# Local attention: maxima subtracted as the bias of eight exponentials per tile instead of by two products on TensorE

## The chip, the core and the metric

The kernel runs on one core of a Trainium2 chip. The metric is the device time of one execution in microseconds (us); the time before is the median of three executions, 1153.07 us (1151.7 to 1158.17). Engines are named as in the profile: PE is TensorE's matmul, PEld its weight load, DVE is VectorE, ACT is ScalarE, POOL is GpSimd, SP is SyncE. L1261 is line 1261 of the kernel before.

## The reference, cut to what matters

A first attention block (16 heads, full softmax over 1024 positions) is followed by two layers that each hold a local attention and a gated MLP. The change lies in the local attention, which is run once in each of the two layers:

```python
def local_attention(q, k, v):          # 8 heads of 64, window 64, sequence 1024, batch 2
    ...
    sim = jnp.einsum('bhwid,bhwjd->bhwij', bq, bk)
    i = bt[:, :, None]
    j = btk[:, None, :]
    mask = (i < j) | (i > j + WINDOW) | (j == -1)
    sim = jnp.where(mask, -jnp.finfo(sim.dtype).max, sim)
    attn = jax.nn.softmax(sim, axis=-1)
    out = jnp.einsum('bhwij,bhwjd->bhwid', attn, bv)
    return out.reshape(b, h, n, d)
```

Each query sees the 128 keys of its own window and the one before it. The softmax of a row needs the row's maximum, the exponentials of the differences and their sum.

## The kernel before

The 2 x 1024 rows are cut into 16 tiles of 128 rows (T = 16). Everything after the first attention block is a software pipeline. `over_tiles` walks through steps; in each step every engine runs its list of stages in the order in which the list is written, and a stage with lag g works on tile (step - g). Nothing else orders the work: an engine is in order, and each stage begins with waits on semaphores that count what other engines have finished.

The local attention of a layer has these lags: `turn_x` 0, `project_qk` and `products` 1, `square` and norms 2, `turn_qk` 3, everything about scores 4, `multiply_v` and `turn_o` 5, `project_out` 6. In one step the engines run, in this order:

- PE: `multiply_qk` (two products of the mask with an identity, L1380, and 32 small score products, L1385), `multiply_v` of the tile before (32 products, L1398), `project_v` (L1411), `shift_scores` (L1418), `project_qk` (L1435), `turn_e` (eight transposes of the exponentials, L1444), `turn_o` (four, L1450), `turn_qk` (eight, L1465), `project_out` (L1474), `turn_x` (L1427).
- ACT: `square` (L1248), `take_v` (L1255), `exponentials` (L1261), `take_eT` (two copies, L1280), `take_oT` (L1296), `take_qkT` (L1286, L1290), `take_hT` (L1271 to L1274).
- DVE: `maxima` (L1317), `normalise`, `weighted`, `square_sums`, `products` (four, L1349), `denominators` (L1354, L1357), `residual` (L1362).

The scores of a tile fill banks 5 and 6 of PSUM: 128 query rows by 8 heads by 128 keys. `maxima` writes the negated maximum of each row and head into `nmax` (128 x 8). `shift_scores` waits for it and adds it to the scores where they lie, by two products that accumulate into the two banks. `exponentials` then waits for `shifted` and turns all 1024 columns in one instruction. `turn_e` waits for `exp_done`, transposes heads 0 to 3 into bank 3 and heads 4 to 7 into bank 4, and `take_eT` copies each bank away once its four transposes are done.

Of the 16 steps of a layer in which scores are computed, the first 13 also have a `project_qk` between `project_v` and `turn_e` (tiles 0 to 12 of the scores); in the last three no projection is left to do. The MLP of a layer starts 17 steps after its attention and overlaps its last steps. Its `gelu` (L1573) has three instructions per tile, each over 128 columns of a PSUM bank, with a bias from an SBUF column and a semaphore of its own.

Of the kernel before, what the change touches and what calls it, by code (L numbers as in the profile page):

```python
# [8 lines left out]
F32R = mybir.dt.float32r  # L9
BF16 = mybir.dt.bfloat16  # L10
ALU = mybir.AluOpType
ACT = mybir.ActivationFunctionType
AX_X = mybir.AxisListType.X

P = 128
B, N, D = 2, 1024, 128
TB = N // P
T = B * TB
# [59 lines left out]
def need(eng, sem, count):  # L78

    if count > 0:  # L80
        eng.wait_ge(sem, count)
# [11 lines left out]
def adaln_block(nc, x, wq, wk, wv, wo, f_wqkv, f_qs, f_ks, f_wo, f_lg, f_lb, f_w1, f_b1, f_w2, f_b2,  # L93
# [7 lines left out]
    with ExitStack() as whole:  # L101
# [919 lines left out]
        mask_b = fsb("mask_b", [P, 2, 2 * WIN], BF16)  # L1021
        ident_b = fsb("ident_b", [P, P], BF16)
        ident_w = fsb("ident_w", [P, 2, WIN], BF16)
        ident_r = fsb("ident_r", [P, P], F32R)
        XS = fsb("XS", [P, T, D // 2])
        buffers = {}

# [43 lines left out]
        with nc.Block() as block:  # L1071
            @block.vector
            def _(dve):
                dve.wait_ge(ld_mask, 16)
                dve.tensor_copy(mask_b[:, :, :], mask[:, :, :])
                dve.tensor_copy(ident_b[:, :], ident[:, :])
                dve.tensor_copy(ident_r[:, :], ident[:, :])
                for w in range(2):
                    half = slice(WIN * w, WIN * w + WIN)
                    dve.tensor_copy(ident_w[half, :, :], ident[half, half][:, None, :].to_broadcast([WIN, 2, WIN]))  # L1080
# [2 lines left out]
        before = {"xf_done": xf_done, "tab_done": tab_done, "res_step": res_step}  # L1083
        for l in range(DEPTH):
            att_sems, attention = local_attention(l, psum, sb, new_sem, dict(before), XF, XA, XS, ident, minus_half,
                                                  fw_qkv, fw_o, xpos[:, l], mask, mask_b, ident_b, ident_w, ident_r)
            before.update(att_sems)
            mlp_sems, mlp = gated_mlp(l, psum, sb, new_sem, dict(before), X, XF, XA, XS, ident, minus_half, fw_1,
                                      fw_2, fb_1, f_ln, rows, out, scale_tables)
            before = {**att_sems, **{name: mlp_sems[name] for name in ("gelu_done", "u_done", "xf_done")}}  # L1090
            parts += [(attention, LAYER_STEPS * l + AHEAD), (mlp, LAYER_STEPS * l + MLP_STEP + AHEAD)]
# [28 lines left out]


def local_attention(l, psum, sb, new_sem, before, XF, XA, XS, ident, minus_half, fw_qkv, fw_o, xpos, mask, mask_b,
                    ident_b, ident_w, ident_r):


    def banks(a, n=1):
        return psum[:, a:a + n, :].rearrange("p b c -> p (b c)")
# [3 lines left out]
    def sem(name):  # L1131
        sems[name] = new_sem(f"{name}_a{l}")
        return sems[name]
# [12 lines left out]
    vp = sb("vp_att", [P, 2, INNER])  # L1146
    qT = sb("qT_att", [P, 2, FH // 2, P])
    kT = sb("kT_att", [P, FH // 2, WIN + N])
    nmax = sb("nmax_att", [P, 2, FH], F32R)
    E = sb("E_att", [P, 2, FH, 2 * WIN])  # L1150
    den = sb("den_att", [P, 2, FH])
    den_inv = sb("den_inv_att", [P, 2, FH])
# [17 lines left out]
    qkT_done = sem("qkT_done")  # L1170
    scores_done = sem("scores_done")
    max_done = sem("max_done")
    shifted = sem("shifted")
    exp_done = sem("exp_done")
    den_done = sem("den_done")
    inv_done = sem("inv_done")
# [63 lines left out]
    def scalar(act):  # L1240
        if l == 0:
            act.wait_ge(cleared, 1)

        def square(t, s):
            need(act, cos_done, 2 * (t + 1))
            need(act, sin_done, 2 * (t + 1))
            need(act, ss_done, t)
            act.activation(sq[:, :, :].rearrange("p h d -> p (h d)"), banks(0, 2), ACT.Square).then_inc(sq_done, 1)  # L1248

        def take_v(t, s):  # L1250
            need(act, v_proj, t + 1)
            need(act, pv_done, t - 1)
            if t > 0:
                act.wait_ge(vp_in[1 - s], 32 * ((t - 1) // 2 + 1))
            act.activation(v[:, s, :], banks(2), ACT.Copy).then_inc(v_done, 1)  # L1255

        def exponentials(t, s):
            need(act, shifted, t + 1)
            need(act, e_turned, 2 * (t - 1))
            need(act, den_done, t - 1)  # L1260
            act.activation(E[:, s].rearrange("p h c -> p (h c)"), banks(5, 2), ACT.Exp).then_inc(exp_done, 1)  # L1261

        def take_hT(t, s):


            need(act, v_proj, t - HR + 1)
            need(act, x_turned, t + 1)
            need(act, hT_done, 3 * t)
            if l > 0 and t == 0:
                act.wait_ge(before["hT_done"], 3 * T)  # L1270
            act.activation(hT[HD:P, t % HR, 0:1], hT[HD:P, (t - 1) % HR, P:P + 1], ACT.Copy,  # L1271
                           scale=0.0 if t % TB == 0 else 1.0).then_inc(hT_done, 1)
            act.activation(hT[0:HD, t % HR, 0:P], ps_x[0:HD, :], ACT.Copy).then_inc(hT_done, 1)
            act.activation(hT[HD:P, t % HR, 1:P + 1], ps_x[HD:P, :], ACT.Copy).then_inc(hT_done, 1)  # L1274

        def take_eT(t, s):
            need(act, pv_done, t - 1)
            for n in range(2):
                need(act, e_turned, 2 * t + n + 1)
                act.activation(ET[:, s, 4 * n:4 * n + 4, :], banks(3 + n).rearrange("p (h c) -> p h c", c=P),  # L1280
                               ACT.Copy).then_inc(eT_done, 1)

        def take_qkT(t, s):
            need(act, qk_turned, 2 * t + 1)
            need(act, scores_done, t - 1)
            act.activation(qT[:, s, :, :], banks(3).rearrange("p (j c) -> p j c", c=P), ACT.Copy)\  # L1286
                .then_inc(qkT_done, 1)
            need(act, qk_turned, 2 * t + 2)
            c0 = WIN + t % TB * P
            act.activation(kT[:, :, c0:c0 + P], banks(4).rearrange("p (j c) -> p j c", c=P), ACT.Copy)\  # L1290
                .then_inc(qkT_done, 1)

        def take_oT(t, s):
            need(act, o_turned, t + 1)
            need(act, out_proj, t - 1)
            act.activation(oT[:, s], banks(7).rearrange("p (j c) -> p j c", c=P), ACT.Copy)\  # L1296
                .then_inc(oT_done, 1)

        return [(square, NORMS), (take_v, SCORES), (exponentials, SCORES), (take_eT, SCORES), (take_oT, PV),
                (take_qkT, TURN_QK), (take_hT, TURN_X)]  # L1300

    def vector(dve):
# [10 lines left out]
        def maxima(t, s):  # L1313

            need(dve, scores_done, t + 1)
            need(dve, shifted, t - 1)
            dve.tensor_reduce(nmax[:, s, :], banks(5, 2).rearrange("p (h c) -> p h c", c=P), AX_X, ALU.max,  # L1317
                              negate=True).then_inc(max_done, 1)

# [29 lines left out]
                    dve.tensor_tensor(dst[:, s, n * FH:(n + 1) * FH, :], ps_qk[n], table, ALU.mult).then_inc(done, 1)  # L1349

        def denominators(t, s):
            need(dve, exp_done, t + 1)
            need(dve, inv_done, t - 1)
            dve.tensor_reduce(den[:, s, :], E[:, s, :, :], AX_X, ALU.add).then_inc(den_done, 1)  # L1354
            need(dve, den_done, t + 1)
            need(dve, o_done, t - 1)
            dve.reciprocal(den_inv[:, s, :], den[:, s, :]).then_inc(inv_done, 1)  # L1357
# [9 lines left out]
    def tensor(pe):  # L1367
        def multiply_qk(t, s):
            need(pe, qkT_done, 2 * (t + 1))
            need(pe, exp_done, t)  # L1370
            if l == 0 and t == 0:
                pe.wait_ge(before["res_step"], 4 * T)
            c0 = t % TB * P
# [37 lines left out]
            pe.matmul(banks(2), hT[:, t % HR, 0:P], fw_qkv[:, l, 2 * INNER:3 * INNER], start=True, stop=True)\  # L1411
                .then_inc(v_proj, 1)

        def shift_scores(t, s):

            need(pe, max_done, t + 1)
            for n in range(2):
                last = pe.matmul(banks(5 + n).rearrange("p (h c) -> p h c", c=P), ident_r[:, :],  # L1418
                                 nmax[:, s, 4 * n:4 * n + 4][:, :, None].to_broadcast([P, FH // 2, P]),
                                 start=False, stop=True, skip_group_check=True)  # L1420
            last.then_inc(shifted, 1)

        def turn_x(t, s):
            pe.wait_ge(before["xf_done"], t + 1)
            need(pe, hT_done, 3 * t)
# [10 lines left out]
                          start=True, stop=True).then_inc(qk_proj, 1)  # L1436

        def turn_e(t, s):
            need(pe, exp_done, t + 1)
            need(pe, qkT_done, 2 * (t + 1))  # L1440
            need(pe, eT_done, 2 * t)
            for n in range(2):
                for j in range(4):
                    last = pe.transpose(banks(3 + n)[:, j * P:(j + 1) * P], E[:, s, 4 * n + j, :], ident[:, :])  # L1444
                last.then_inc(e_turned, 1)
# [22 lines left out]
        def project_out(t, s):  # L1468
# [4 lines left out]
            for j in range(FH // 2):  # L1473
# [1 line left out]
                                 stop=(j == FH // 2 - 1))  # L1475
            last.then_inc(out_proj, 1)

        return [(multiply_qk, SCORES), (multiply_v, PV), (project_v, SCORES), (shift_scores, SCORES),
                (project_qk, PROJECT), (turn_e, SCORES), (turn_o, PV), (turn_qk, TURN_QK), (project_out, OUT),
                (turn_x, TURN_X)]  # L1480

# [3 lines left out]
def gated_mlp(l, psum, sb, new_sem, before, X, XF, XA, XS, ident, minus_half, fw_1, fw_2, fb_1, f_ln, rows, out,  # L1485
# [3 lines left out]
    def banks(a, n=1):  # L1489
        return psum[:, a:a + n, :].rearrange("p b c -> p (b c)")  # L1490
# [126 lines left out]
    def tensor(pe):  # L1617
        def turn_x(t, s):
            need(pe, xn_done, 2 * (t + 1))
            need(pe, hT_done, t - 1)  # L1620
            need(pe, gelu_done, HC * (t - 1))
            if t < 2:

                pe.wait_ge(before["eT_done"], 2 * T)
                pe.wait_ge(before["exp_done"], T)
            pe.transpose(ps_x(s), xn[:, s, :], ident[:, :]).then_inc(x_turned, 1)

        def hidden(t, s):
# [49 lines left out]
```

## Time and profile before

| | |
|---|---|
| median of three executions | 1153.07 us (1151.7 to 1158.17) |
| profiled execution, its own time | 1154.28 us |
| its span, first to last instruction | 1152.5 us |
| mean granted TensorE clock | 0.973 of full speed |
| local attention of layer 0, scores of first to last tile | 768.9 to 903.8 us |
| local attention of layer 1, the same | 965.2 to 1099.7 us |

The profile is of one execution. Busy times of engines overlap, so they don't add up to the span; what sets the time of a stage is read from who waits for whom. A matmul's record reaches until its result has drained, so that the start of the next group on PE says more about PE's pace than the end of the one before.

### The profile page before, as it was taken

How to read it: one execution, taken by the hardware profiler on the slowest of the kernel's cores; microseconds unless marked ns; L12 is line 12 of the kernel's file. 1: busy time of each engine (PE TensorE's matmuls, PEld its weight loads, DVE VectorE, ACT ScalarE, POOL GpSimd, SP SyncE). 2: the span in 40 equal slices, each digit the busy share in tenths (PEclk: the TensorE clock that was granted, in tenths of full speed). 3: DMA queues.
4: the chain of work that ended last, by engine and by line, in shares of the span. 5: the costliest groups of instructions: out<-in, count | busy, mean ns of one | idle time of the engine just before them, and what ended most of it. 6: DMA issues, size and time to landing. Idle time of an engine off the chain costs nothing. (4 is left out here: it accounts for less than half of the span.)

```text
span 1152.5 us, 22995 instructions
## 1 busy us (share of the span) xinstructions
PE 1072.7 (93%) x8352; PEld 666.0 (58%) x8352; DVE 828.5 (72%) x1522; ACT 633.2 (55%) x1000; POOL 750.5 (65%) x511
## 2 busy tenths in 40 slices
PE   6884899999999999999999999779999898999988
PEld 4552455455454554445545555747777695777677
DVE  6994666666666666666666663579998689888867
ACT  2442356666665565655656564036666455666554
POOL 3662465767677676867667778389986337666526
PEclk8996799999999999999999999889999999999999
DMA  8899621533315243142242100101111100111111
GB/s 257 270 267 354 159 48 48 110 75 83 75 47 111 52 87 89 49 102 59 60 100 65 48 11 20 56 10 31 33 37 37 26 2 15 36 32 33 33 26 36
DMA packets 83456, 89.03 MB, mean 77 GB/s; under 512 B 32740, under 2 KB 66064, under 8 KB 83344
## 3 DMA queue, kind: packets, MB, share of 16 engines
q1 hardware_dynamic: 83344, 87.55, 29.5%
q8 instruction: 68, 1.11, 0.4%
q14 instruction: 44, 0.36, 0.1%
HBM read 53.57 MB, written 24.25 MB: 68 GB/s over the span
## 5 line engine op out<-in xcount | busy, mean ns | idle before, releaser
L863 DVE CUSTOM_DVE_ANT_0 junk<-psum,alibi 128x1024 bf16<-128x1024 f32 x256 | 313.2, 1223 | 205.1 <-PE psum L918 196.8
L834 ACT ACTIVATE E<-psum,keybias_sb 128x1024 f32<-128x1024 f32 x256 | 274.9, 1113 | 234.7 <-PE psum L942 221.4
L767 POOL TENSOR_TENSOR sum_p<-sum_p,E 128x1024 f32<-128x1024 f32 x96 | 232.4, 2421 | 96.2 <-ACT E L834 91.8
L954 PE MATMUL psum<-E,V 128*64 128x512 f32 x1024 | 248.7, 606 | 0.0
L918 PE MATMUL psum<-KH,QH 64*128 64x512 f32 x512 | 118.6, 459 | 12.0 <-PEq L275 6.9
L954 PEld LDWEIGHTS psum<-E,V 128*64 128x64 f32 x1024 | 62.2, 136 | 112.2 <-issue 98.3
L773 POOL TENSOR_TENSOR sum_p<-sum_p,xpos_sb 128x1024 f32<-128x1024 f32 x32 | 76.2, 2382 | 69.0 <-DVE xpos_sb L873 69.0
L918 PEld LDWEIGHTS psum<-KH,QH 64*128 64x128 f32 x512 | 49.4, 189 | 121.5 <-DVE M L863 84.6
L942 PE MATMUL psum<-QH,KH 64*128 64x512 f32 x512 | 102.8, 397 | 5.9 <-DMA QM<-mrow 3.9
L942 PE MATMUL psum<-QL,KH 64*128 64x512 f32 x512 | 101.6, 392 | 0.0
L942 PE MATMUL psum<-QH,KL 64*128 64x512 f32 x512 | 101.4, 392 | 0.0
L942 PE MATMUL psum<-QM,one_rows 64*128 64x512 f32 x512 | 101.2, 390 | 0.0
L1226 POOL TENSOR_TENSOR rinv_att<-ss_up_att,minus_half 128x16 f32<-128x16 f32 x32 | 93.6, 2925 | 2.7
L1349 DVE TENSOR_TENSOR t_att<-psum,xpos_sb 128x512 f32<-128x512 f32 x128 | 79.1, 678 | 1.7 <-PE psum L1435 1.7
L767 POOL TENSOR_TENSOR sum_p<-E 128x1024 f32<-128x1024 f32 x32 | 76.5, 2390 | 5.2 <-POOL sum_p L773 5.1
L1435 PE MATMUL psum<-fw_qkv,hT_att 128*128 128x512 f32 x128 | 61.9, 607 | 6.3 <-ACT sq_att L1248 5.0
L942 PEld LDWEIGHTS psum<-QH,KH 64*128 64x128 f32 x512 | 48.5, 186 | 18.2 <-DMA QM<-mrow 8.3
L1317 DVE TENSOR_REDUCE nmax_att<-psum 128x8 fp32r<-128x1024 f32 x32 | 39.2, 1225 | 26.7 <-PE psum L1385 26.6
L942 PEld LDWEIGHTS psum<-QH,KL 64*128 64x128 f32 x512 | 48.7, 185 | 10.9
L942 PEld LDWEIGHTS psum<-QM,one_rows 64*128 64x128 f32 x512 | 48.5, 185 | 11.1
L942 PEld LDWEIGHTS psum<-QL,KH 64*128 64x128 f32 x512 | 48.6, 185 | 10.5
L1255 ACT ACTIVATE v_att<-psum 128x512 f32<-128x512 f32 x32 | 19.1, 597 | 63.5 <-PE psum L1411 63.5
(148 smaller groups left out, 2072.5 us busy)
## 6 DMA issues: line engine op xcount, KB each, us to landing
QH<-qa_scratch SPq DMA_DIRECT2D x64, 256.0 KB, 4.2
qa_scratch<-tH SPq DMA_DIRECT2D x8, 1024.0 KB, 5.6
qa_scratch<-tL SPq DMA_DIRECT2D x8, 1024.0 KB, 7.9
QL<-qa_scratch SPq DMA_DIRECT2D x64, 128.0 KB, 4.2
XF<-inverse_scratch SPq DMA_DIRECT2D x32, 256.0 KB, 3.4
vp_att<-v_att SPq DMA_DIRECT2D x64, 128.0 KB, 2.3
KH<-k_scratch SPq DMA_DIRECT2D x16, 256.0 KB, 4.0
KL<-k_scratch SPq DMA_DIRECT2D x16, 256.0 KB, 5.3
```

What stands on the lines that cost most here:

```text
L767: pool.tensor_tensor(sum_p[:, s, :], first, E[:, k % 4, :], ALU.add)\
L773: pool.tensor_tensor(sum_p[:, s, :], sum_p[:, s, :], sum_d[:, s, :], ALU.add)\
L834: act.activation(E[:, k % 4, :], scores(k % 2), ACT.Exp, bias=kb).then_inc(exp_done, 1)
L863: dve.tensor_tensor_reduce(junk[:, :], banks(max_bank(i, k), 2), alibi[:, s, :], -1.0, BIG, ALU.add, ALU.min, M[:, s, k:k + 1]).then_inc(m ...
L918: last = pe.matmul(banks(max_bank(i, k) + ch), QH[rows, s, k * P:(k + 1) * P], KH[rows, g, ch * 512:(ch + 1) * 512], start=True, stop=True)
L942: last = pe.matmul(scores(k % 2)[:, ch * 512:(ch + 1) * 512], key[rows], query[rows, a:a + 512], start=(n == 0), stop=(n == len(terms) - 1))
L954: last = pe.matmul(banks(6 + i % 2)[HD * ch:HD * ch + HD, :], V[:, g, k, :], E[:, k % 4, ch * 512:(ch + 1) * 512], start=(k == 0), stop=(k ...
L1226: pool.tensor_tensor(rinv[:, s, :], ss_up[:, s, :], minus_half[:, 0:NH], ALU.pow)\
L1255: act.activation(v[:, s, :], banks(2), ACT.Copy).then_inc(v_done, 1)
L1317: dve.tensor_reduce(nmax[:, s, :], banks(5, 2).rearrange("p (h c) -> p h c", c=P), AX_X, ALU.max, negate=True).then_inc(max_done, 1)
L1349: dve.tensor_tensor(dst[:, s, n * FH:(n + 1) * FH, :], ps_qk[n], table, ALU.mult).then_inc(done, 1)
L1435: pe.matmul(banks(n), hT[:, t % HR, 0:P], fw_qkv[:, l, n * INNER:(n + 1) * INNER], start=True, stop=True).then_inc(qk_proj, 1)
```

## The change

The two products of `shift_scores` go, with the stage, its semaphore and the identity in its format (`ident_r`, one copy on DVE at 736 us). `exponentials` waits for the maxima themselves and runs once per head, eight instructions of 128 columns, each with the head's column of `nmax` as its bias. `exp_done` counts heads now, and `turn_e` waits for it twice: for the first four heads before its first four transposes, for all eight before the last four. Other waits on `exp_done` are multiplied by eight. `nmax` is plain float32.

```diff
         def exponentials(t, s):
-            need(act, shifted, t + 1)
+            need(act, max_done, t + 1)
             need(act, e_turned, 2 * (t - 1))
             need(act, den_done, t - 1)
-            act.activation(E[:, s].rearrange("p h c -> p (h c)"), banks(5, 2), ACT.Exp).then_inc(exp_done, 1)
+            for n in range(FH):
+                act.activation(E[:, s, n, :], banks(5, 2)[:, n * P:(n + 1) * P], ACT.Exp,
+                               bias=nmax[:, s, n:n + 1]).then_inc(exp_done, 1)
...
         def maxima(t, s):
             need(dve, scores_done, t + 1)
-            need(dve, shifted, t - 1)
+            need(dve, exp_done, FH * (t - 1))
...
         def denominators(t, s):
-            need(dve, exp_done, t + 1)
+            need(dve, exp_done, FH * (t + 1))
...
         def multiply_qk(t, s):
             need(pe, qkT_done, 2 * (t + 1))
-            need(pe, exp_done, t)
+            need(pe, exp_done, FH * t)
...
-        def shift_scores(t, s):
-
-            need(pe, max_done, t + 1)
-            for n in range(2):
-                last = pe.matmul(banks(5 + n).rearrange("p (h c) -> p h c", c=P), ident_r[:, :],
-                                 nmax[:, s, 4 * n:4 * n + 4][:, :, None].to_broadcast([P, FH // 2, P]),
-                                 start=False, stop=True, skip_group_check=True)
-            last.then_inc(shifted, 1)
...
         def turn_e(t, s):
-            need(pe, exp_done, t + 1)
             need(pe, qkT_done, 2 * (t + 1))
             need(pe, eT_done, 2 * t)
             for n in range(2):
+                need(pe, exp_done, FH * t + 4 * (n + 1))
                 for j in range(4):
                     last = pe.transpose(banks(3 + n)[:, j * P:(j + 1) * P], E[:, s, 4 * n + j, :], ident[:, :])
                 last.then_inc(e_turned, 1)
```

## Rows read from the trace of the kernel before

**Rows 1.** The page: busy time by engine, share of the span.

```profile
PE 1072.7 (93%) x8352; PEld 666.0 (58%) x8352; DVE 828.5 (72%) x1522; ACT 633.2 (55%) x1000; POOL 750.5 (65%) x511
```

**Rows 2.** Chain of work, 849.8 to 858.9: start, us, what.

```profile
849.84 1.03 PE psum L1385 x32
...
853.01 0.43 PE psum L1418 x2
...
858.82 0.25 PE psum L1385
```

**Rows 3.** Windows, three steps: PE, PEld, DVE, ACT, POOL busy, PEclk, DMA.

```profile
849.77:858.75 8.98, 8.98 (x105) 6.63 (x103) 8.09 (x12) 5.83 (x12) 8.22 (x8) 1.00 0.17 37
1018.63:1027.62 8.99, 8.99 (x105) 6.63 (x104) 7.97 (x13) 5.84 (x12) 5.66 (x5) 1.00 0.16 36
885.60:894.15 8.55, 7.38 (x100) 5.73 (x99) 5.93 (x10) 4.59 (x8) 5.31 (x4) 1.00 0.16 35
```

**Rows 4.** Timeline, one full step: start, us, engine, idle before and releaser.

```profile
849.77 1.10 PE L1385 MATMUL psum<-kT_att,qT_att 64*64 64x128 f32 x32
849.82 0.27 ACT L1273 ACTIVATE hT_att<-psum 64x128 f32<-64x128 f32 x1
...
850.12 0.28 ACT L1274 ACTIVATE hT_att<-psum 64x128 f32<-64x128 f32 x1
...
850.94 1.23 DVE L1317 TENSOR_REDUCE nmax_att<-psum 128x8 fp32r<-128x1024 f32 x1 [0.63 <-PE psum L1385]
...
853.05 0.60 ACT L1255 ACTIVATE v_att<-psum 128x512 f32<-128x512 f32 x1 [1.60 <-PE psum L1411]
...
853.54 1.02 ACT L1261 ACTIVATE E_att<-psum 128x1024 f32<-128x1024 f32 x1
...
854.99 1.04 PE L1444 MATMUL psum<-ident,E_att 128*128 128x128 f32 x8
...
855.69 1.09 ACT L1280 ACTIVATE ET_att<-psum 128x512 f32<-128x512 f32 x2 [1.13 <-PE psum L1444]
...
855.87 0.60 PE L1450 MATMUL psum<-ident,O_att 128*128 128x128 f32 x4
...
857.41 1.20 DVE L1354 TENSOR_REDUCE den_att<-E_att 128x8 f32<-128x1024 f32 x1
```

**Rows 5.** Timeline, one of the three late steps without a projection.

```profile
885.60 1.10 PE L1385 MATMUL psum<-kT_att,qT_att 64*64 64x128 f32 x32
...
889.38 1.02 ACT L1261 ACTIVATE E_att<-psum 128x1024 f32<-128x1024 f32 x1
...
890.45 1.09 PE L1444 MATMUL psum<-ident,E_att 128*128 128x128 f32 x8 [1.17 <-ACT E_att L1261]
...
891.20 1.09 ACT L1280 ACTIVATE ET_att<-psum 128x512 f32<-128x512 f32 x2 [0.81 <-PE psum L1444]
...
891.38 0.60 PE L1450 MATMUL psum<-ident,O_att 128*128 128x128 f32 x4
```

**Rows 6.** Groups by form: count, busy us, mean ns of one, idle before.

```profile
L834 ACT ACTIVATE E<-psum,keybias_sb 128x1024 f32<-128x1024 f32 x256 | 274.9, 1113 | 234.7 <-PE psum L942 221.4 <-DVE xpos_sb L873 13.3
L1261 ACT ACTIVATE E_att<-psum 128x1024 f32<-128x1024 f32 x32 | 32.6, 1018 | 0.0
L1573 ACT ACTIVATE gate_mlp<-psum,fb 128x128 f32<-128x128 f32 x64 | 20.0, 364 | 31.2 <-PE psum L1635 31.2
```

**Rows 7.** Timeline of ACT in the MLP, three Gelus and what follows.

```profile
932.90 0.87 ACT L1573 ACTIVATE gate_mlp<-psum,fb 128x128 f32<-128x128 f32 x3 [1.02 <-PE psum L1635]
933.68 0.46 ACT L1566 ACTIVATE hT_mlp<-psum,f_ln 128x128 f32<-128x128 f32 x1
```

**Rows 8.** Windows around gaps of PE, columns as in Rows 3.

```profile
765.00:770.00 5.00, 4.30 (x35) 3.07 (x39) 3.68 (x6) 2.96 (x6) 4.83 (x6) 0.52 0.00 0
910.00:915.00 5.00, 3.41 (x51) 3.16 (x52) 2.41 (x9) 1.75 (x3) 1.47 (x3) 1.00 0.04 8
```

**Rows 9.** Chain of work at 769, the first score step of layer 0.

```profile
768.92 1.91 PE psum L1385 x32
```

More of the change, by code:

```diff
@@ L1023, in adaln_block @@
         ident_w = fsb("ident_w", [P, 2, WIN], BF16)
-        ident_r = fsb("ident_r", [P, P], F32R)
         XS = fsb("XS", [P, T, D // 2])
@@ L1076, in _ @@
                 dve.tensor_copy(ident_b[:, :], ident[:, :])
-                dve.tensor_copy(ident_r[:, :], ident[:, :])
                 for w in range(2):
@@ L1085, in adaln_block @@
             att_sems, attention = local_attention(l, psum, sb, new_sem, dict(before), XF, XA, XS, ident, minus_half,
-                                                  fw_qkv, fw_o, xpos[:, l], mask, mask_b, ident_b, ident_w, ident_r)
+                                                  fw_qkv, fw_o, xpos[:, l], mask, mask_b, ident_b, ident_w)
             before.update(att_sems)
@@ L1122, in local_attention @@
 def local_attention(l, psum, sb, new_sem, before, XF, XA, XS, ident, minus_half, fw_qkv, fw_o, xpos, mask, mask_b,
-                    ident_b, ident_w, ident_r):
+                    ident_b, ident_w):
     def banks(a, n=1):
@@ L1148, in local_attention @@
     kT = sb("kT_att", [P, FH // 2, WIN + N])
-    nmax = sb("nmax_att", [P, 2, FH], F32R)
+    nmax = sb("nmax_att", [P, 2, FH])
     E = sb("E_att", [P, 2, FH, 2 * WIN])
@@ L1172, in local_attention @@
     max_done = sem("max_done")
-    shifted = sem("shifted")
     exp_done = sem("exp_done")
@@ L1476, in project_out @@
             last.then_inc(out_proj, 1)
-        return [(multiply_qk, SCORES), (multiply_v, PV), (project_v, SCORES), (shift_scores, SCORES),
+        return [(multiply_qk, SCORES), (multiply_v, PV), (project_v, SCORES),
                 (project_qk, PROJECT), (turn_e, SCORES), (turn_o, PV), (turn_qk, TURN_QK), (project_out, OUT),
@@ L1624, in turn_x @@
                 pe.wait_ge(before["eT_done"], 2 * T)
-                pe.wait_ge(before["exp_done"], T)
+                pe.wait_ge(before["exp_done"], FH * T)
             pe.transpose(ps_x(s), xn[:, s, :], ident[:, :]).then_inc(x_turned, 1)
```

## The prediction

> **What bounds the kernel now.** I read the page first. PE is busy 93% of the span and ACT 55% [rows 1]. That suggests a good trade, but both are averages over stages with different limits. So I went to the stage of the change, to its windows by step. In a step with all stages PE is busy 8.98 of 8.98 us and ACT 5.83; a step of layer 1 shows the same. In the late steps, where no `project_qk` is left, PE is busy 7.38 of 8.55 us [rows 3]. Then the chain of work: in a full step every piece is PE's, the two shifting products hold it for 0.43 us, and from one step's score products to the next it takes 8.98 us [rows 2].
>
> The timeline shows how much cover there is. I count from S, the start of L1385. ACT waits 1.60 us for `project_v`, copies v at S + 3.28 and starts the exponentials at S + 3.77, although the maxima are there at S + 2.40: it is `take_v`, ahead in ACT's queue, that holds the exponentials, not the shift. They end 0.43 us before PE comes to `turn_e` (S + 5.22), and `turn_o` starts at S + 6.10 [rows 4]. In a late step that cover is missing: PE waits 1.17 us for the exponentials, goes on 0.05 us after their end, and `turn_o` starts at S + 5.78 [rows 5].
>
> **The change, part by part.**
>
> *Removed from PE:* two products, 0.43 us a step [rows 2]. In a full step that is on the chain. In a late step it lies in PE's wait and is worth nothing.
>
> *Removed before the exponentials:* the wait for `shifted` becomes one for `max_done`, which comes earlier. Worth nothing: `take_v` still ends where it ended, as `project_v` stands before the shift in PE's list. The exponentials start at S + 3.77 as before.
>
> *Added on ACT:* seven more instructions, and a bias. The nearest row for one of them is the Gelu of the MLP: 128 x 128, PSUM to SBUF, bias from a column, a semaphore each, 364 ns [rows 6]. The bias is in line with that: 1113 ns against 1018 ns for 1024 columns [rows 6]. What counts is the distance from start to start. Three Gelus are followed by the next instruction 0.78 us after the first began (933.68 - 932.90) [rows 7], so 0.26 us each; I use 0.258, which is between this and what the 0.87 us of the three give ((0.87 - 0.36) / 2 = 0.255). Eight exponentials then end 7 x 0.258 + 0.364 = 2.17 us after they start, against 1.02. ACT has room for the 1.15 us (5.83 of 8.98 busy), but PE waits for their end.
>
> *When PE can go on:* the fourth exponential ends at 3.77 + 3 x 0.258 + 0.364 = S + 4.91. PE, without its shift, gets there at 5.22 - 0.43 = 4.79, and waits briefly. The eighth ends at 3.77 + 2.17 = S + 5.94, 0.05 us later PE goes on with the second half. In the late step, all eight transposes took from 890.45 to 891.38, 0.93 us, until `turn_o` started [rows 5]; four take 4 x 0.11 = 0.44 less (eight take 0.88 in a stream [rows 4]), so 0.49 us. `turn_o` starts at 5.94 + 0.05 + 0.49 = S + 6.48.
>
> *The sum of a step:* full, 6.48 - 6.10 = 0.38 us longer, with the 0.43 already given back; late, 6.48 - 5.78 = 0.70 us longer.
>
> *What follows in the step:* ACT's first `take_eT` can start at 3.77 + 8 x 0.258 = S + 5.83, before 5.92. The second has to wait for the second half of the transposes: 0.75 us after PE resumes (891.20 - 890.45) [rows 5], S + 6.74 against 5.92 + 0.49 = 6.41 (the two copies last 1.09). So ACT's copies are 0.33 us late, less than PE's 0.38: oT, qT and kT come no later for PE than before, and the delay neither grows nor is made up. The scores of the next step start that much later. DVE's denominators start at S + 7.64 and have 1.7 us to spare [rows 4]; in late steps they wait for the exponentials anyway and shift with them.
>
> *At no cost:* the copy into `ident_r` (one, of 0.22 us, among DVE's short ones before the pipeline starts); the format of `nmax`; the multiplied waits, which ask for the same events; the wait of `maxima` on `exp_done` of two tiles back, long past. SP and POOL are not touched.
>
> *Total:* 13 full and 3 late steps in each of two layers. 26 x 0.38 + 6 x 0.70 = 9.9 + 4.2 = 14.1 us. The first two score steps of a layer have PE waiting on ACT's copies as well; I give them the 0.38 too. Against the profiled execution, 1154.28 + 14.1 = 1168.4; it was 1.2 us above the median, so the median should be 1153.07 + 14.1, some 1167 us.
>
> **The bounds of the unknown.** No row shows an exponential of 128 columns. From below: 1018 ns for 1024 columns without bias is at least 0.127 us of passage per 128 columns; eight at that distance would give the full gain, but the short instructions that the rows show begin 0.26 and 0.30 us before their successors [rows 4, 7]. From above: the two copies of 64 x 128 take 0.27 us and start 0.30 us apart, without overlap [rows 4]; if biased exponentials behave so, the distance is 0.364 + 0.025 = 0.39. The Gelu is by far the nearest in form, so I take 0.258. Each 0.01 us of distance moves a step by 0.07, the whole by 2.2 us.
>
> The Gelus overlap their successor by about 0.1 us and take 364 ns [rows 6, 7]. The Trainium skill, "ScalarE: Activation LUTs", section "What ACT_TABLE_LOAD costs", gives 280 ns + 0.833 ns per column with a bias pointer and an overlap of 93 ns: 387 ns each and 0.294 apart. An estimate by that page is 7 x 0.036 + 0.023 = 0.275 us more a step, 8.8 us in all, and 1176 us. It speaks against the change more strongly than the row does, in the same direction.
>
> **The rivals.**
>
> *Faster: the exponentials stay hidden and PE keeps its 0.43 us.* For it: ACT idles 1.60 us before v and 1.13 us before the transposes in each full step [rows 4]. Against it: the first gap lies before `take_v`, which the exponentials can't pass, and the second ends at `turn_e`. It pays off below the distance at which 26 (x - 6.10) + 6 (x - 5.78) = 0: x = 6.04, so 7p + 0.364 = 6.04 - 0.54 - 3.77 and p = 0.195 (0.203 if the end shrinks with it). The full gain is 26 x 0.43 = 11 us, 1142 us; at most 4 in 100.
>
> *The same:* a distance of 0.17 to 0.22 us, within 5.8 us of before. 7 in 100.
>
> *Exponentials back to back without overlap,* at 0.39 us like the copies: `turn_o` at 3.77 + 2.73 + 0.36 + 0.54 = S + 7.40; 26 x 1.30 + 6 x 1.62 = 43.5 us, 1197 us. For it, those copies; against it, the Gelus. 5 in 100.
>
> *PE's clock falls.* A full step would have PE idle about 0.8 us in two gaps. Where the clock was granted at half, the score products took 1.91 us instead of 1.03 [rows 2, 9]; for a whole step I put 2 us, and two such stretches in each layer beyond the forecast give 1175 us. For it: a clock of 0.52 in the window from 765 us, where a layer begins [rows 8]. Against it: late steps already idle 1.17 us of 8.55 at a clock of 1.00 [rows 3], and so does a window with PE busy 3.41 of 5 us [rows 8]. 4 in 100.
>
> *The distance is 0.30 us,* that of the two copies of 64 rows [rows 4]: 7 x 0.042 = 0.29 us a step more than forecast, 32 x 0.29 = 9.4 us, 1177 us. For it: an exponential may start up more slowly than a Gelu, which no row compares; against it: 1018 ns for 1024 columns shows nothing slow in it [rows 6]. 15 in 100. The page of the Trainium skill named above gives nearly the same.
>
> **How the numbers follow.** The forecast, slower by 8 to 19 us, gets 65 in 100. The range that holds 8 in 10 reaches from a distance of 0.235 (1161) to slightly above 0.30 (1178); it leaves out the fast cases and those without overlap. A measurement of this kernel tells about 0.5%, 5.8 us, from no change. Slower: 65 + 15 + 5 + 4 = 89; the same 7; faster 4.
>
> **What would show it.** In the profile of the changed kernel: 256 exponentials of about 364 ns, ACT's busy time up by 32 x 1.15 = 37 us; the exponentials' first start still at S + 3.77; PE waiting twice at L1444, about 0.2 and 0.5 us, both ended by `E_att`; a full step of 9.36 us and a late one of 9.25; clock 1.00. Wrong would be a step of 8.55 us (hidden after all), a start of the exponentials before v's copy, or a wait of PE on kT in place of E (then ACT's queue as a whole has become the bound, which would add to the 0.38).

## The result, and the profile after

The changed kernel takes 1174.39 us (median of six, 1169.89 to 1176.04) against 1153.48 us before (six executions). The medians lie 20.9 us apart; the ratio is 1.0168, 95% interval 1.0139 to 1.0198, by which it is 19.4 us. I had put 1167, with a range of 1161 to 1178, so the time lies in the range and on its far side. (Of all the runs below, one execution, of experiment 4, went at a mean clock of 0.575 and took 1707 us; it is left out.) The profiled execution has a span of 1174.2 us against 1152.5 before, 21.7 us more.

The page of the changed kernel shows the trade that was made (busy time by engine, then the groups of the exponentials and of the transposes that need them; the last column is the idle time in front of them):

```profile
PE 1072.3 (91%) x8288; PEld 657.8 (56%) x8288; DVE 830.9 (71%) x1521; ACT 673.1 (57%) x1224; POOL 749.5 (64%) x511
...
L1259 ACT ACTIVATE E_att<-psum,nmax_att 128x128 f32<-128x128 f32 x256 | 69.4, 384 | 0.6
L1434 PE MATMUL psum<-ident,E_att 128*128 128x128 f32 x256 | 41.8, 287 | 28.1 <-ACT E_att L1259 28.1
```

Beside [rows 1], PE has 64 instructions fewer and is busy for the same time; ACT is busy 39.9 us longer, where I had said 37, and the exponentials are 69.4 - 32.6 = 36.8 us of it [rows 6]. The last figure is the price: PE sits idle 28.1 us in front of the transposes. The same group of the kernel before has 7.3 us:

```profile
L1444 PE MATMUL psum<-ident,E_att 128*128 128x128 f32 x256 | 33.6, 274 | 7.3 <-ACT E_att L1261 7.3
```

The windows of the changed kernel: two full steps, one late step, the two late steps that have become longest, and a stretch of the MLP of layer 0 (columns as in the windows before).

```profile
870.99:880.37 9.38, 8.84 (x104) 6.17 (x102) 8.10 (x11) 7.09 (x19) 5.64 (x5) 1.00 0.14 31
1032.70:1042.09 9.39, 8.85 (x104) 6.17 (x102) 8.09 (x11) 7.10 (x19) 5.66 (x5) 1.00 0.15 33
900.40:909.54 9.14, 7.02 (x99) 5.35 (x97) 5.14 (x11) 5.21 (x14) 1.50 (x3) 1.00 0.16 35
889.64:900.40 10.76, 8.64 (x98) 7.01 (x97) 5.80 (x9) 6.06 (x15) 4.97 (x4) 0.84 0.13 30
1107.51:1118.26 10.75, 8.63 (x99) 7.01 (x97) 5.13 (x11) 5.53 (x14) 0.79 (x2) 0.84 0.13 30
920.00:925.00 5.00, 4.21 (x44) 4.02 (x43) 0.69 (x1) 1.62 (x3) 1.47 (x3) 0.50 0.05 11
```

A full step is 9.38 us where it was 8.98, a late one 9.14 where it was 8.55 [rows 3]. The fourth and fifth rows are late steps as well, but 1.6 us longer, and TensorE's granted clock in them is 0.84: part of the step ran at half speed, 1.2 instead of 2.4 GHz. In the last row the clock is at half for the whole window.

The timeline of one full step of the changed kernel (start, us, engine, idle before and releaser):

```profile
870.99 1.10 PE L1384 MATMUL psum<-kT_att,qT_att 64*64 64x128 f32 x32
...
874.27 0.60 ACT L1252 ACTIVATE v_att<-psum 128x512 f32<-128x512 f32 x1 [1.61 <-PE psum L1410]
...
874.89 2.17 ACT L1259 ACTIVATE E_att<-psum,nmax_att 128x128 f32<-128x128 f32 x8
...
876.17 0.63 PE L1434 MATMUL psum<-ident,E_att 128*128 128x128 f32 x4 [0.23 <-ACT E_att L1259]
...
877.11 0.66 PE L1434 MATMUL psum<-ident,E_att 128*128 128x128 f32 x4 [0.31 <-ACT E_att L1259]
...
877.60 0.60 PE L1440 MATMUL psum<-ident,O_att 128*128 128x128 f32 x4
```

Read it against [rows 4]. With S = 870.99, v is copied at S + 3.28 as before. The eight exponentials take 2.17 us, to the hundredth what I had worked out, but begin at S + 3.90, not 3.77. PE waits twice. The second half of the transposes resumes 0.05 us after the last exponential, and `turn_o` starts 0.49 us after that, at S + 6.61 (before 6.10). The next S comes 2.77 us later, where before it took 2.88: PE no longer waits 0.1 us for the first copy of the transposes before `turn_qk`.

**Where the 21.7 us lie.** I took the start of the score products in each of the 32 steps of both traces and subtracted.

| stretch | longer by, us | forecast |
|---|---|---|
| 26 steps with a projection | 4.0 + 5.4 = 9.4 | 9.9 |
| six late steps at 9.14 instead of 8.55 | 3.5 | 4.2 |
| two late steps, above their 9.14 | 3.2 | 0 |
| from layer 0's last late step to layer 1, beyond that step's 0.59 | 4.0 | 0 |
| the same at the end of layer 1 | 1.5 | 0 |

The first row includes 0.8 us in the kernel's favour: the first score step of layer 0 took 8.30 us instead of 9.11, with less of it at half clock than before [rows 9]. So 12.9 us are the steps, and 8.7 us lie where the granted clock is at half. The 4.0 us can be placed closely. In layer 0's last late step the clock falls at 916.2 us and is back at 926.5. Product by product, PE runs 0.7 us behind the kernel before at 915.7 and 4.6 us behind at 926.9, and the 4.6 us stay until layer 1 begins.

### The profile page after: what moved, and what is told of

The parts are those of the page before. It is cut to its first block and busy times, and to the rows that moved or that the text cites. A ratio compares the mean times of both kernels' runs of the same rounds, so it can differ in the third digit from the quotient of the medians.

```text
span 1174.2 us, 23090 instructions
## 1 busy us (share of the span) xinstructions
PE 1072.3 (91%) x8288; PEld 657.8 (56%) x8288; DVE 830.9 (71%) x1521; ACT 673.1 (57%) x1224; POOL 749.5 (64%) x511
## 5 line engine op out<-in xcount | busy, mean ns | idle before, releaser
L1259 ACT ACTIVATE E_att<-psum,nmax_att 128x128 f32<-128x128 f32 x256 | 69.4, 384 | 0.6
L1434 PE MATMUL psum<-ident,E_att 128*128 128x128 f32 x256 | 41.8, 287 | 28.1 <-ACT E_att L1259 28.1
L1316 DVE TENSOR_REDUCE nmax_att<-psum 128x8 f32<-128x1024 f32 x32 | 39.1, 1222 | 32.3 <-PE psum L1384 32.3
L1434 PEld LDWEIGHTS psum<-ident,E_att 128*128 128x128 f32 x256 | 27.2, 142 | 61.2 <-issue 43.6
```

Source lines behind the costliest of these rows:

```text
L1259: act.activation(E[:, s, n, :], banks(5, 2)[:, n * P:(n + 1) * P], ACT.Exp, bias=nmax[:, s, n:n + 1]).then_inc(exp_done, 1)
```

## The experiments

All times are medians, ratios are against the kernel before on the same chip, with 95% intervals. The diffs show the lines that matter; where the number of exponentials changes, the counts in all waits on `exp_done` change with it. An S is again the start of a step's score products.

**1. The saving without the cost: no products, one exponential without bias.** The maxima are computed and not subtracted.

```diff
-            for n in range(FH):
-                act.activation(E[:, s, n, :], banks(5, 2)[:, n * P:(n + 1) * P], ACT.Exp,
-                               bias=nmax[:, s, n:n + 1]).then_inc(exp_done, 1)
+            act.activation(E[:, s].rearrange("p h c -> p (h c)"), banks(5, 2), ACT.Exp).then_inc(exp_done, 1)
```

> The two shifting products are left out and the single exponential of 1024 columns is kept, without bias: the maxima are computed but not subtracted. This is the saving of the change without its cost. Theory A: PE gets its 0.43 us a full step back, less what it then waits for the exponential (end at S + 4.79, where PE arrives): full step about 8.6 us, late step unchanged at 8.55, the whole 1153 - 26 x 0.38 = about 1143 us. Theory B (another engine bounds the full step at about 8.98 us anyway, so the products were worth nothing): 1153 us.

1146.33 us, ratio 0.9938 (0.9918 to 0.9958). The full step is 8.66 us, the late one 8.55. So the two products were worth 0.33 of their 0.43 us in each full step and nothing in a late one, as theory A has it. The whole is 3 us above the 1143 expected, and 2 us of that are steps of layer 0: its second takes 9.29 us and its fifth 9.57, where PE waits for the output of the tile before. DVE makes it late, as it waited itself for POOL:

```profile
806.54 2.22 DVE L1320 TENSOR_TENSOR qk_att<-qk_att,rinv_att 128x1024 f32<-128x1024 f32 x1 [0.99 <-POOL rinv_att L1223]
...
809.42 0.66 PE L1438 MATMUL psum<-ident,O_att 128*128 128x128 f32 x4 [0.85 <-DVE O_att L1329]
```

So with the products gone, DVE and POOL are the next bound in layer 0's first steps.

**2. The eight exponentials without their bias.** The edit to the changed kernel is `bias=nmax[:, s, n:n + 1]` left out; the maxima are not subtracted.

> The changed kernel with eight exponentials per tile but without their bias (the maxima are computed but not subtracted). It tells what costs, the number of instructions or the bias. Theory A1 (the count: each instruction keeps ACT for about 0.25 us from start to start whatever its operands): the eight still take about 2.1 us, full step 9.3 us, the whole 1171 to 1174 us. Theory A2 (the bias: without it 128 columns take 0.28 us and start 0.16 us apart): the eight take 1.4 us, end at S + 5.1, full step about 8.6 to 8.7 us, the whole about 1148 us.

1143.48 us, ratio 0.9916 (0.9896 to 0.9937). This is A2, and it corrects how one would tell the story: eight instructions instead of one are cheap. From its groups and its timeline:

```profile
L1259 ACT ACTIVATE E_att<-psum 128x128 f32<-128x128 f32 x256 | 46.8, 318 | 0.0
```

```profile
876.16 0.60 ACT L1252 ACTIVATE v_att<-psum 128x512 f32<-128x512 f32 x1 [1.60 <-PE psum L1409]
876.66 1.46 ACT L1259 ACTIVATE E_att<-psum 128x128 f32<-128x128 f32 x8
...
877.68 1.15 PE L1433 MATMUL psum<-ident,E_att 128*128 128x128 f32 x8
```

The eight last 1.46 us and the last of them 0.37, so they start (1.46 - 0.37) / 7 = 0.16 us apart, against (2.17 - 0.41) / 7 = 0.25 with the bias. Of the 1.15 us that the change added on ACT, 0.44 are thus the split and 0.71 the bias. PE comes to the transposes at S + 4.80 and the profile counts no wait in front of them; the full step is 8.55 us, the full 0.43 less. It is even 0.11 us a step below experiment 1: `turn_o` starts at S + 5.78 in both, but the first four transposes are done earlier, ACT's first copy of them starts at S + 5.49 instead of 5.59, and `turn_qk` at 6.24 instead of 6.34.

The Trainium skill, "ScalarE: Activation LUTs", section "What ACT_TABLE_LOAD costs", says that a pointer operand adds about 93 ns to an instruction; the difference of 0.09 us here agrees. With bias the trace has 0.25 apart, not the 0.294 worked out from the page's figures.

**3. The split alone, in the kernel before.** Products kept, its exponential in eight without bias, `turn_e` waiting by halves.

```diff
-            act.activation(E[:, s].rearrange("p h c -> p (h c)"), banks(5, 2), ACT.Exp).then_inc(exp_done, 1)
+            for n in range(FH):
+                act.activation(E[:, s, n, :], banks(5, 2)[:, n * P:(n + 1) * P], ACT.Exp).then_inc(exp_done, 1)
```

> The kernel before, products kept, with its exponential split into eight without bias and turn_e waiting by halves as in the changed kernel. Splitting alone. Theory A: the eight take 1.46 us as in the run without bias, so in a full step they end at S + 5.2, just as PE comes to turn_e (S + 5.22), and the first half is there long before: full step 8.98 us as before, late step 0.1 us shorter or the same (8.44 to 8.55): 1152 to 1153 us, no change. Rival (the split itself costs PE a wait): 1158 us or more.

1153.02 us, ratio 0.9993 (0.998 to 1.0007). Full step 8.98 us, late step 8.43. No change, as expected.

**4. Half the biased instructions.** Four exponentials of 256 columns; two heads share the first one's bias, so the second head's maximum isn't its own.

```diff
-            for n in range(FH):
-                act.activation(E[:, s, n, :], banks(5, 2)[:, n * P:(n + 1) * P], ACT.Exp,
-                               bias=nmax[:, s, n:n + 1]).then_inc(exp_done, 1)
+            for n in range(0, FH, 2):
+                act.activation(E[:, s, n:n + 2, :].rearrange("p h c -> p (h c)"),
+                               banks(5, 2)[:, n * P:(n + 2) * P], ACT.Exp,
+                               bias=nmax[:, s, n:n + 1]).then_inc(exp_done, 1)
```

> The changed kernel with four biased exponentials of 256 columns instead of eight of 128 (two heads share the bias of the first, so the second head's maximum is not its own). A dose: half the instructions with a bias. Theory A with the distance that the changed kernel showed (0.249 us, plus 0.107 for 128 columns more): they end 3 x 0.356 + 0.50 = 1.57 us after they start, S + 5.47 in a full step, and PE goes on with the second half then: full step 9.38 - 0.60 = 8.78 us, late step 9.14 - 0.60 = 8.54 us, the whole near 1148 us. Rival (the step is set by something else that the change brought, such as the second wait or the order): like the changed kernel, 1170 us or more.

1147.92 us, ratio 0.9946 (0.9929 to 0.9963). The same kernel once more, for its steps:

> The kernel with four biased exponentials once more, since its profile was taken in a disturbed execution while its timed runs gave 1147 to 1150 us. For its steps: full step 8.78 us and late step 8.54 us by theory A; above 9.2 us by the rival.

1147.61 us, ratio 0.9936 (0.9916 to 0.9956). Its windows, a full and a late step:

```profile
1012.59:1021.37 8.78, 8.77 (x103) 6.17 (x102) 7.97 (x11) 6.60 (x15) 5.66 (x5) 1.00 0.16 36
1082.58:1091.12 8.54, 7.02 (x99) 5.34 (x97) 5.14 (x11) 4.72 (x10) 0.87 (x3) 1.00 0.17 37
```

8.78 and 8.54 us, the numbers of theory A. Half the dose takes the whole loss away: with four the end of the exponentials comes at S + 5.47, and PE has turned its first half just before.

**5. One wait instead of two.**

```diff
             for n in range(2):
-                need(pe, exp_done, FH * t + 4 * (n + 1))
+                need(pe, exp_done, FH * (t + 1))
```

> The changed kernel with turn_e waiting for all eight heads before its first transpose, not for four and then for eight. Theory A (PE is gated by the end of the eighth): the second half's 0.49 us becomes 0.93, so each of the 32 steps is 0.44 us longer, full 9.82 and late 9.58 us, the whole 14 us above the changed kernel, near 1188 us. Rival (the copies of the transposes on ACT are the gate, and those begin after the eight exponentials anyway): less than half of that, under 1181 us.

1196.87 us, ratio 1.0368 (1.0338 to 1.0399). Full step 10.01 us, late step 9.76 at full clock. The direction is A's, the size is 0.6 us a step, not 0.44. `turn_o` starts 0.5 us later than in the changed kernel (S + 7.12 against 6.61) and from there to the next S it takes 2.89 us, the 2.88 of the kernel before and not the 2.77 of the changed one. I had left that out: ACT's first copy comes after the transposes again, and by the lengths `turn_qk` waits for it again. Over 32 steps the 0.6 us are 20 of the 22.5 that the kernel becomes slower; in four of the six late steps, where PE now waits 2.85 us, the clock falls as well (one takes 12.46 us at 0.73).

**6. The clock: idle products in the late steps.** PE repeats the last projection's products there, into banks nobody reads any more.

```diff
+        def fill_late(t, s):
+            if t < T - 3:
+                return
+            need(pe, sq_done, T)
+            need(pe, cos_done, 2 * T)
+            need(pe, sin_done, 2 * T)
+            for n in range(2):
+                pe.matmul(banks(n), hT[:, (T - 1) % HR, 0:P], fw_qkv[:, l, n * INNER:(n + 1) * INNER],
+                          start=True, stop=True)
...
-                (project_qk, PROJECT), (turn_e, SCORES), (turn_o, PV), (turn_qk, TURN_QK), (project_out, OUT),
+                (project_qk, PROJECT), (fill_late, SCORES), (turn_e, SCORES), (turn_o, PV), (turn_qk, TURN_QK), (project_out, OUT),
```

> The changed kernel plus idle work: in the three late steps of each layer PE repeats, between project_v and turn_e, the products of the last project_qk into banks that nobody reads any more (four of 0.43 us, into the time in which it waits for the exponentials). Theory C (what the result has beyond my forecast, some 8 us, is the clock that falls to half because PE waits more in the late steps): no late step of 10.8 us, mean clock up, the whole 5 to 9 us below the changed kernel, about 1167 us. Rival: the clock falls for another reason or costs nothing on the path, and the added work shows: equal to the changed kernel or up to 3 us slower.

1168.95 us (1167.53 to 1169.84), ratio 1.0135 (1.0116 to 1.0153): 5.4 us less than the changed kernel by the medians, for work that nobody needs. By the ratios it is 3.8 us, and their intervals overlap, but each of the four executions is below each of the changed kernel's six. The profile shows where it comes from. The same late steps:

```profile
891.46:900.60 9.14, 8.74 (x102) 6.10 (x101) 5.80 (x9) 5.75 (x15) 4.98 (x4) 1.00 0.16 35
900.60:909.74 9.14, 8.74 (x103) 6.11 (x101) 5.14 (x11) 5.21 (x14) 1.50 (x3) 1.00 0.16 35
```

PE is busy 8.74 instead of 7.02 us, the clock stays at 1.00, every late step is 9.14 us, and from the last one of layer 0 to the first score step of layer 1 it takes 61.8 us instead of 67.0. The clock in the late steps was a cost of its own. Other runs fit: where PE waits 1.60 us before the transposes of a late step (experiment 1) or 1.69 (experiment 10), the clock is 1.00 through all late steps of the profile; in the changed kernel it falls in four of the six, and so it does with 2.85 us (experiment 5). Two things stay open. Why a late step of the changed kernel loses its clock and another, with the same waits, doesn't, these runs don't show. And not all of the 8.7 us need be the change's: in experiments 1, 8 and 9 the clock is at half for 3.4 us as well, 9 to 11 us after the start of layer 0's last score step. The changed kernel's own executions go the same way: of the six, two took 1176.0 us at a mean clock of 0.967 and 0.969, two 1169.9 us at 0.972 and 0.974.

**7. The order on ACT: exponentials ahead of the copy of v,** in the changed kernel.

```diff
-        return [(square, NORMS), (take_v, SCORES), (exponentials, SCORES), (take_eT, SCORES), (take_oT, PV),
+        return [(square, NORMS), (exponentials, SCORES), (take_v, SCORES), (take_eT, SCORES), (take_oT, PV),
```

> The changed kernel with one edit: ACT runs the eight exponentials of a tile before it copies v, not after. Theory A (the end of the exponentials gates turn_e, and take_v ahead of them in ACT's queue is what makes them late): they start once the maxima are there, about S + 2.45 us after the start of the score products, end at S + 4.62, and PE, without its shift, comes to turn_e at S + 4.79 and waits no more. Full step 8.55 to 8.65 us instead of 9.38, late step about 7.9 instead of 9.14, the whole near 1140 us. Theory B (ACT's queue as a whole, or DVE with 8.1 us busy a step, bounds the step as soon as ACT has eight instructions more): full step stays above 8.9 us, the whole at 1153 us or more. Theory C (most of the loss is TensorE's clock in the late steps): the clock shows no stretch at half in them only if PE's waits there shrink; both A and C expect that here.

1141.77 us, ratio 0.9903 (0.9883 to 0.9923). From the timeline:

```profile
872.00 1.10 PE L1384 MATMUL psum<-kT_att,qT_att 64*64 64x128 f32 x32
...
874.43 2.17 ACT L1259 ACTIVATE E_att<-psum,nmax_att 128x128 f32<-128x128 f32 x8 [0.76 <-DVE nmax_att L1316]
...
876.44 0.65 ACT L1252 ACTIVATE v_att<-psum 128x512 f32<-128x512 f32 x1
```

The same 2.17 us of biased exponentials now begin at S + 2.43, when the maxima are there. Full steps are mostly 8.55 us, late ones 7.93. ACT is busy as long as in the changed kernel; B falls, though DVE does bound some of the steps. In layer 1 some full steps are 8.57 to 8.64 us with DVE busy 8.58 of 8.61, and its first late step is 8.62 us, as DVE delivers the maxima late. In layer 0 four of the first six steps take 8.7 to 9.4 us; in the longest PE waits 0.79 us for DVE's output, as in experiment 1. Together that is some 3 us, enough for the step from 1140 to 1142.

**8. The order alone,** in the kernel before, products kept (the same edit).

> The kernel before with one edit: ACT runs its exponential before it copies v. Was the order alone worth the time that it brought to the changed kernel? Theory A: no. In a full step PE is busy throughout and the exponential was hidden already, full step 8.98 us; in a late step the shifting products still stand behind project_v on PE, so it starts at S + 3.7 instead of 3.78, 0.1 us less: 1152 to 1153 us, the same as before. Rival (the order alone gives the gain): 1145 us or less.

1152.54 us, ratio 0.9991 (0.9979 to 1.0002). Full step 8.98 us, late step 8.49. The order is worth nothing as long as the products stand between the maxima and the exponentials and PE is full.

**9. One maximum for the eight heads of a row, and the order.**

```diff
-    nmax = sb("nmax_att", [P, 2, FH])
+    nmax = sb("nmax_att", [P, 2, 1])
...
-            for n in range(FH):
-                act.activation(E[:, s, n, :], banks(5, 2)[:, n * P:(n + 1) * P], ACT.Exp,
-                               bias=nmax[:, s, n:n + 1]).then_inc(exp_done, 1)
+            act.activation(E[:, s].rearrange("p h c -> p (h c)"), banks(5, 2), ACT.Exp,
+                           bias=nmax[:, s, :]).then_inc(exp_done, 1)
...
-            dve.tensor_reduce(nmax[:, s, :], banks(5, 2).rearrange("p (h c) -> p h c", c=P), AX_X, ALU.max,
+            dve.tensor_reduce(nmax[:, s, :], banks(5, 2), AX_X, ALU.max,
```

> No products, exponentials ahead of the copy of v, and one maximum for the eight heads of a row in place of one per head: a softmax may subtract any number that is the same for a head's row, as long as no head's own maximum lies so far below that its exponentials vanish. One biased exponential of 1024 columns, 1.11 us. Theory A: it ends at S + 2.45 + 1.11 = 3.6, long before PE comes to turn_e in a full step (8.55 us, PE bound), and 0.5 us after it does in a late one (about 7.3 us instead of 7.93): 1136 to 1140 us, the fastest. Rival (the full step at 8.55 us is already bound by PE and the late ones by DVE or the copies): equal to the version with eight exponentials ahead of the copy of v, 1142 us.

1136.75 us, ratio 0.9841 (0.9824 to 0.9857), the fastest of all. Two windows of it, a full and a late step:

```profile
865.38:873.93 8.55, 8.55 (x103) 6.25 (x101) 8.50 (x12) 5.92 (x12) 5.57 (x5) 1.00 0.16 35
890.05:897.36 7.31, 6.95 (x99) 5.36 (x97) 5.05 (x11) 4.16 (x7) 3.95 (x4) 1.00 0.19 44
```

The late step is 7.31 us, as expected (the first of each layer 7.67 and 8.44), and in the full one DVE (8.50 of 8.55 us) is now as full as PE. The shared maximum rests on the data: computed from the reference with its own inputs, a head's maximum lies at most 9.2 below the row's largest, where an exponential in float32 is far from vanishing. For inputs with a far wider spread between heads it would not do.

**10. The shared maximum without the order.**

> The fastest version so far without its change of order: no products, one biased exponential of 1024 columns with one maximum for the eight heads of a row, after the copy of v. It separates the two things that this version joined. Theory A: the exponential ends at S + 3.9 + 1.11 = 5.0, PE is there at 4.79: full step 8.98 - 0.43 + 0.2 = about 8.75 us, late step 8.55 + 0.1 = 8.64 us: 1148 us. Rival (the count of instructions alone mattered, the order nothing): 1137 us as the joint version.

1151.69 us, ratio 0.9979 (0.9967 to 0.9992). Late step 8.64 us as expected, full step 8.89, not 8.75: the exponential ends at S + 5.02, PE goes on at S + 5.07, is at `turn_o` at S + 6.00, and the wait at `turn_qk` is back as in experiment 5. So of the 17 us of the joint version the order brings 15, once the products are gone, and it brings nothing while they are there.

## Why the prediction was right, and what it missed

- *What holds the exponentials is `take_v`, and their end gates PE.* Right. Experiment 7 moves their start and turns a loss of 21 us into a gain of 11; experiments 4 and 5 move their end, or the point at which PE waits for it, and the steps follow. The profile counts 0.23 and 0.31 us for PE's two waits in a full step, where I had said 0.2 and 0.5: it counts from the end of a record, and from start to start the second is 0.5 us.
- *The products are worth 0.43 us in a full step and nothing in a late one.* Right (experiments 1 and 2: 0.33 and 0.43; 8.55 us in a late step of experiment 1).
- *The distance from start to start, 0.258 us.* It was 0.25, and the eight took 2.17 us as worked out. That it fits to the hundredth is luck: the seven distances together are 0.05 us shorter than I had put them, and the last instruction is 0.05 us longer (0.41, not 0.364). That the Gelu was the right row to take, and not the instruction without bias, is what the sum hangs on: at 0.16 us the kernel takes 10 us less than before (experiment 2). My sentence on what is added named "seven more instructions, and a bias" in one breath. The seven instructions alone cost PE nothing (experiment 3: 0.44 us more on ACT, the same step); a bias on each is what costs.
- *`turn_o` at S + 6.48.* In late steps exactly that, in full steps 6.61, as the exponentials begin 0.13 us later there. Against this I had missed a gain of 0.11 us: before, PE had waited for the first copy of the transposes ahead of `turn_qk`, and now that copy is early. A full step became 0.40 us longer, not 0.38; a late one 0.59, not 0.70, for the same 0.11.
- *The sum of the steps, 14.1 us.* Measured 12.9, or 13.7 without the first score step of layer 0, whose gain of 0.8 us is the clock's.
- *The range.* That it holds the time is luck in part. Its upper end, 1178, was made for a distance of 0.30 us, which didn't come; what filled it was the clock, for which it was not made. (At 2.2 us for each 0.01 the lower end is 1162, not 1161.)
- *The rival of the clock, 4 in 100.* This is the step that failed: the sum puts the clock at nothing. I set it aside because late steps of the kernel before idle 1.17 of 8.55 us at a clock of 1.00, and looked for PE's new waits in the full steps, where the clock stayed at 1.00. But in the changed kernel PE idles in a late step 1.81 + 0.31 = 2.1 of 9.14 us, and in two such steps, and again from within each layer's last one, the clock fell to half. That is 8.7 us in the profiled execution; idle work in the late steps gave back 5.4 us of the median (experiment 6), and whether the rest is the change's stays open. The rival's time, 1175 us, was the one that came, by the forecast's mechanism and the clock together. The row at hand bounded the wait of before, not the one that followed for after from my own working: in a late step the fourth exponential at S + 4.91 and PE free 0.43 us earlier.
- *The fast rival* would have come true under another order on ACT, which the text had named as the reason against it.

## What to carry to other kernels

Before work is moved from a full engine to one that is half idle, look at where the idle engine's gaps lie and who waits for the end of its new work: 5.83 of 8.98 us busy said nothing, while `take_v` in front of the exponentials said all. Then try the order of the queue: the same change with two entries of a list swapped went from 1.7% slower to 1.0% faster. When a prediction itself lengthens PE's waits in a stretch, check the clock against the predicted waits, not against the old ones.

## What the hardware showed that I had not expected

- A bias from an SBUF column costs ACT 0.09 us, not only in the length of an instruction but in the distance to the next one: 0.25 against 0.16 us for 128 columns. For one instruction of 1024 columns it costs 0.1 us in all (1113 ns in experiment 10 against 1018).
- In the steps with a projection (all 26 but the one with a table load in between) the first biased exponential begins 0.62 us after the copy of v, in the late steps 0.49, as before the change. Without a bias it is 0.49 in both (experiment 2), and a single biased exponential has the same 0.62 and 0.49 (experiment 10). Idle products on PE in the late steps don't bring the 0.13 us there (experiment 6), so PE's projection alone doesn't bring it. What it is stays open; it is worth 25 x 0.13 = 3.3 us.
- Four products of 0.43 us that serve nothing, put into a wait of PE, made the kernel 5.4 us faster by the medians (experiment 6).
